# One address layout for the adjacency matrices of a graph and MoE kernel: half columns written into full rows

## The chip, the cores and the metric

The kernel runs on one core of a Trainium2 chip. The metric is the device time of one execution in microseconds (us). Three timed runs of the kernel before gave 2316.9, 2317.39 and 2327.94 us, median 2317.39 us.

## The reference

A graph of 3125 nodes with 256 features and 100000 weighted edges goes through four blocks. Cut to what matters here:

```python
# block 1, twice: aggregate over weighted edges
agg = segment_sum(edge_weight[:, None] * x[src], dst, num_segments=n)
x = gelu(layer_norm((x + agg) @ W + b))
# block 2: dense FFN with 4 small experts, top 2 gated (no edges)
# block 3: two GCN convolutions, over the edges with self loops
deg = segment_sum(ones, dst); dinv = rsqrt(deg)
out = segment_sum((x @ W)[src] * (dinv[src] * dinv[dst])[:, None], dst) + b
# block 4: 8 experts, top 2 gated, width 256 (no edges)
```

The edges come sorted by `dst`, and `dst` is drawn so that low node numbers have more edges.

## The kernel before, in words

The kernel turns the edge list into two dense matrices in device memory: `weight_matrix` (sums of edge weights from source node to destination node, plus one on the diagonal) and `count_matrix` (numbers of edges, plus one on the diagonal). Aggregation is then a dense matrix product on TensorE: all 25 tiles of 128 source nodes against a block of destination columns.

**The build.** The 3200 (padded) destination columns are made in 20 units of 160 columns (`UCOLS`). For each unit TensorE adds up one-hot products in PSUM (L1337, L1338), with one-hots that VectorE makes in batches (L980 to L985). ScalarE copies the sums in ten groups from PSUM to a staging buffer in SBUF (L560) and sets the PSUM banks back to zero (L564). GpSimd adds the diagonal (L821) and keeps a copy of the degree row (L823). Then SyncE (SP) issues two DMAs (L473), one for each matrix, of 128 partitions by 25 tiles by 160 columns of four bytes, 16000 bytes in each partition. There are two staging buffers, called halves: even units use half 0 and odd units half 1. Before ScalarE copies unit u into its half, `stage_free` has it wait until both DMAs of unit u-2 have landed. So unit u, its diagonal, its write and unit u+2 form one loop.

**The streaming.** Three passes read the matrices back, two over the weights and one over the counts. A pass has 10 steps of 320 columns (`SUB`, which is two units side by side). The 25 tiles of a step come in five DMAs (L506, for the very first step L476) into a ring of five slots of 5 tiles each. A slot is loaded again as soon as TensorE has used it, and TensorE comes back to it four slots later. TensorE multiplies each tile, 128 by 320, into two PSUM banks (L1401); each fp32 product is two instructions in the trace, 100 instructions in a step.

In device memory the layout before is [step, half, partition, tile, 160]. A unit's write is one unbroken piece for each partition (16000 bytes). A ring load needs two pieces of 3200 bytes for each partition, one from each half, and the SBUF slot keeps the halves apart: [half, tile, 160]. The moving operand of L1401 is then two runs of 160 columns that lie 3200 bytes apart.

**Between the two.** After the last unit, SP writes it, waits for the writes, and loads the ring for step 1; step 0 has been loaded beforehand. ScalarE issues some 60 DMAs for the weights of the model (L600) once the first ring loads have landed. After that it turns the degrees into the scaling values (L608, GpSimd L830, L611), for which TensorE waits before it goes on with the first pass (L1460).

Of the kernel before, what the change touches and what calls it, by code (L numbers as in the profile page):

```python
# [16 lines left out]
F32 = mybir.dt.float32  # L17
# [3 lines left out]
ds = bass.ds  # L21

P = 128
NODES = 3125
TILES = -(-NODES // P)
# [7 lines left out]
SUPERS = TILES // SUPER  # L33
SCOLS = SUPER * P
SUB = SCOLS // 2
QUADS = 5
UNITS = TILES // QUADS
# [15 lines left out]
UCOLS = SUB // 2  # L53
# [59 lines left out]
def build_program(nc, a, out):  # L113
    with ExitStack() as ctx:
# [4 lines left out]
            return ctx.enter_context(nc.semaphore(name))  # L119


        weight_dram = nc.dram_tensor("weight_matrix", [2 * SUPERS, 2, P, TILES, UCOLS], F32).ap()
        count_dram = nc.dram_tensor("count_matrix", [2 * SUPERS, 2, P, TILES, UCOLS], F32).ap()


        x_nodes = sb("x_nodes", [P, TILES, D])
        act_a = sb("act_a", [P, TILES, D])
        act_c = sb("act_c", [P, KD, PADDED])
        wide = sb("wide", [P, 18400])
        ring = wide[:, 0:8000].rearrange("p (a h b c) -> p a h b c", a=UNITS, h=2, b=QUADS)  # L130
        act_b = wide[:, 8000:14400].rearrange("p (t f) -> p t f", t=TILES)
        work = wide[:, 14400:18400]
        dinv_row = sb("dinv_row", [P, PADDED])
# [11 lines left out]
        cols = sb("cols", [P, 32])  # L145
# [64 lines left out]
        ps = ctx.enter_context(nc.psum_tensor("ps", [P, 8, 512], F32))  # L210
# [37 lines left out]
        stage = [wide[:, half * ROWS * UCOLS:(half + 1) * ROWS * UCOLS].rearrange("p (r c) -> p r c", r=ROWS) for half in range(2)]  # L248
# [210 lines left out]
        def _(sp):  # L459
# [9 lines left out]
            stage_end(sp, 1)  # L469

            def write(u2, half):
                for matrix, rows_of, written in ((weight_dram, slice(0, TILES), weights_written), (count_dram, slice(TILES, 2 * TILES), counts_written)):
                    sp.dma_start(matrix[ds(u2, 1), half, :, :, :].rearrange("a p t c -> (a p) t c"), stage[half][:, rows_of, :]).then_inc(written[half], 16)  # L473

            def first_unit(q):
                sp.dma_start(ring[:, q, :, :, :], weight_dram[0, :, :, q * QUADS:(q + 1) * QUADS, :].rearrange("h p t c -> p h t c")).then_inc(ring_ready[q], 16)  # L476
            with sp.Fori(0, BUNITS // 2 - 1) as u2:
                for half in range(2):
                    sp.wait_ge(unit_complete, u2 * 2 + half + 1)
# [15 lines left out]
            for k in range(PASSES):  # L495
                matrix = weight_dram if k < 2 else count_dram
                if k == 0:
                    for half in range(2):
                        sp.wait_ge(weights_written[half], 16 + 16 * BUNITS // 2)
                if k == 2:  # L500
                    for half in range(2):
                        sp.wait_ge(counts_written[half], 16 + 16 * BUNITS // 2)
                with sp.Fori(1 if k == 0 else 0, 2 * SUPERS) as u:
                    for q in range(UNITS):
                        sp.wait_ge(ring_used, (k * 2 * SUPERS + u) * UNITS + q + 1)
                        sp.dma_start(ring[:, q, :, :, :], matrix[ds(u, 1), :, :, q * QUADS:(q + 1) * QUADS, :].rearrange("a h p t c -> p (a h) t c")).then_inc(ring_ready[q], 16)  # L506
                if k == PASSES - 1:

                    sp.wait_ge(ffn_out, SUPERS)
                    for e in range(MOES):  # L510
                        sp.dma_start(moe_w2[:, e, :, :], a["L1_ffn_w2"][e].rearrange("(k p) n -> p k n", p=P)).then_inc(moe_w2_loaded, 16)
# [773 lines left out]
        def _(pe):  # L1285
# [98 lines left out]
            def stream(k, s, sub, q):  # L1384

                features = (act_a, act_b, act_b)[k]
                u = (k * SUPERS + s) * 2 + sub
# [10 lines left out]
                    pe.wait_ge(gcn_in, SUPER + (q + 1) * SUPER)  # L1398
                for t in range(QUADS):
                    for h in range(KD):  # L1400
                        i = nc.tensor.matmul(ps[:, 2 * sub + h, 0:SUB], features[:, q * QUADS + t, h * P:(h + 1) * P], ring[:, q, :, t, :],  # L1401
                                             start=q == 0 and t == 0, stop=q == UNITS - 1 and t == QUADS - 1)
                i.then_inc(ring_used, 1)

# [235 lines left out]
```

## Time and profile before

| | value |
|---|---|
| profiled execution | 2316.9 us, span 2315.2 us |
| granted TensorE clock, mean | 0.946 of full speed |
| TensorE busy | 2043.1 us (88%) |
| VectorE busy | 967.8 us (42%) |
| ScalarE busy | 579.4 us (25%) |
| GpSimd busy | 327.0 us (14%) |
| DMA | 70912 packets, 221.10 MB |
| build of the matrices | about 115 us to 729 us |
| first step of the first pass starts | 727.08 us |

The profile is of one execution. A share of busy time is a mean over stages with different limits: here the build has every engine partly busy, and the stages after it have TensorE nearly always busy. Idle time of an engine is listed with the instruction that ended it. "issue" in the chain of waits is time in which an engine waited for nothing that the trace shows. ACTq and SPq are the instruction queues of ScalarE and SyncE, from which they issue DMAs.

### The profile page before, as it was taken

The page shows a single profiled execution, that of the slowest core. Times are in us where ns is not written, and L with a number is a line of the kernel's source. Part 1 is how long each engine was busy: PE and PEld are TensorE (multiplying, and loading weights), DVE is VectorE, ACT ScalarE, POOL GpSimd, SP SyncE. Part 2 cuts the span into 40 slices and gives each one's busy share as a digit, 9 for nine tenths or more (in the row PEclk, how much of TensorE's full clock was granted, in tenths as well). Part 3 has the DMA queues.
Part 4 walks back from the last instruction along what each step waited for, and adds up shares of the span by engine and source line. Part 5 has one row for each costly group of instructions (what it writes and reads, how often), then busy time and mean ns, then how long its engine had stood idle before and what let it go on. Part 6 is the DMA issues. An engine that isn't in the chain of part 4 may idle for free.

```text
span 2315.2 us, 32368 instructions
## 1 busy us (share of the span) xinstructions
PE 2043.1 (88%) x11135; PEld 1584.2 (68%) x11136; DVE 967.8 (42%) x1977; ACT 579.4 (25%) x833; POOL 327.0 (14%) x158
## 2 busy tenths in 40 slices
PE   1688588777666899999999989999999999999997
PEld 1488477777665677777777766656777767777776
DVE  5999598978781011111332332221322233222222
ACT  0014356667663200000101112330000012222221
POOL 2007363445651000000000000000000000000000
PEclk7799799989888899999999998999999998999999
DMA  2000333443348544444434420004344330000000
GB/s 76 1 0 0 142 142 148 171 177 142 142 171 318 147 136 139 140 141 139 128 114 127 122 90 0 0 0 120 122 127 119 122 101 1 12 12 0 11 11 10
DMA packets 70912, 221.10 MB, mean 96 GB/s; under 512 B 10300, under 2 KB 27354, under 8 KB 65754
## 3 DMA queue, kind: packets, MB, share of 16 engines
q1 hardware_dynamic: 56554, 213.41, 26.7%
q10 hardware_dynamic: 14320, 7.18, 1.3%
q8 instruction: 25, 0.41, 0.1%
q14 instruction: 13, 0.11, 0.0%
HBM read 135.45 MB, written 85.12 MB: 95 GB/s over the span
## 4 chain that ended last, share of the span: by engine, by line
issue 57%; PE 25%; DVE 7%; POOL 3%; DMA 3%; ACT 2%; ACTq 1%; DVEq 1%; SPq 0%; POOLq 0%
PE ps L1570 8%; PE ps L1418 8%; PE ps L1337 6%; DVE act_c L985 3%; DMA count_matrix<-wide 3%; POOL wide L821 2%; PE ps L1338 2%; ACT wide L560 1%; PE ps L1312 1%; ACT ps L564 1%; POOL dinv_row L823 1%; DVE act_c L980 1%; ACTq L552 1%; PE ps L1594 1%; DVE wide L1274 0%
## 5 line engine op out<-in xcount | busy, mean ns | idle before, releaser
L1337 PE MATMUL ps<-early,act_c 128*128 128x200 bf16 x3600 | 464.4, 258 | 159.4 <-ACT ps L564 87.3
L1401 PE MATMUL ps<-wide 128*128 128x320 f32 x2000 | 545.3, 433 | 0.0
L1401 PEld LDWEIGHTS ps<-wide 128*128 128x128 f32 x2000 | 378.4, 190 | 153.5 <-issue 0.3
L1337 PEld LDWEIGHTS ps<-early,act_c 128*128 128x128 bf16 x3600 | 338.7, 100 | 189.8 <-issue 184.3
L1338 PE MATMUL ps<-early,act_c 128*128 128x208 bf16 x1200 | 313.0, 261 | 0.0
L821 POOL TENSOR_TENSOR wide<-wide,ident 128x128 f32 (+3 forms) x80 | 242.4, 3058 | 372.0 <-ACT ps L564 371.1
L985 DVE TENSOR_TENSOR act_c<-act_c,pair_tab 128x1024 bf16<-128x1024 bf16 x450 | 282.4, 679 | 0.0
L1401 PE MATMUL ps<-wide,act_a 128*128 128x320 f32 x1000 | 274.0, 436 | 2.1 <-ACTq L585 2.1
L1401 PEld LDWEIGHTS ps<-wide,act_a 128*128 128x128 f32 x1000 | 191.6, 192 | 81.9 <-issue 4.7
L560 ACT COPY wide<-ps 128x816 f32<-128x816 f32 x200 | 167.3, 837 | 283.5 <-PE ps L1338 192.0
L1274 DVE SCALAR_TENSOR_TENSOR wide<-ps,small,wide 128x256 f32<-128x256 f32 x200 | 82.0, 477 | 267.5 <-PE ps L1418 267.4
L1082 DVE TENSOR_TENSOR wide<-ps,rows 128x1280 f32<-128x1280 f32 x10 | 14.9, 1492 | 419.3 <-PE ps L1418 419.3
L1570 PE MATMUL ps<-act_a,wide 128*128 (+1 forms) x640 | 189.7, 452 | 0.0
L835 POOL TENSOR_TENSOR small<-small 128x5 f32<-128x5 f32 x25 | 29.2, 1166 | 1099.5 <-DVE small L1070 1099.5
L1418 PE MATMUL ps<-early,act_c 128*128 128x256 f32 x800 | 182.1, 383 | 2.3 <-DVEq L1276 2.3
L1418 PEld LDWEIGHTS ps<-early,act_c 128*128 128x128 f32 x800 | 153.8, 193 | 28.0 <-issue 2.7
L564 ACT ACTIVATE ps<-ones 128x816 f32<-128x816 f32 x200 | 170.6, 853 | 6.4
L738 ACT ACTIVATE act_c<-ps,cols 128x320 f32<-128x320 f32 x160 | 84.3, 527 | 322.7 <-PE ps L1570 322.7
L1570 PEld LDWEIGHTS ps<-act_a,wide 128*128 128x128 f32 x640 | 126.0, 199 | 54.4 <-issue 11.2
L981 DVE TENSOR_TENSOR early<-rows 128x1600 bf16<-128x1600 bf16 x150 | 146.8, 979 | 0.0
L980 DVE TENSOR_TENSOR act_c<-rows,pair_tab 128x1024 bf16<-128x1024 bf16 x150 | 102.0, 680 | 93.3 <-PE ps L1338 91.9
L1338 PEld LDWEIGHTS ps<-early,act_c 128*128 128x128 bf16 x1200 | 119.9, 100 | 1.7
(195 smaller groups left out, 1318.5 us busy)
## 6 DMA issues: line engine op xcount, KB each, us to landing
wide<-weight_matrix SPq DMA_DIRECT2D x100, 800.0 KB, 4.5
weight_matrix<-wide SPq DMA_DIRECT2D x20, 2000.0 KB, 6.2
count_matrix<-wide SPq DMA_DIRECT2D x20, 2000.0 KB, 10.8
wide<-count_matrix SPq DMA_DIRECT2D x50, 800.0 KB, 4.4
x_nodes<-in_x_dram ACTq DMA_DIRECT2D x1, 3072.0 KB
out_dram<-x_nodes SPq DMA_DIRECT2D x4, 640.0 KB
early<-in_L_ffn_w_dram SPq DMA_DIRECT2D x8, 256.0 KB, 5.3
wide<-in_L_ffn_w_dram SPq DMA_DIRECT2D x8, 256.0 KB, 4.5
```

Of the source, the lines that this page charges most:

```text
L560: act.copy(stage[half][:, :, k * GCOLS:(k + 1) * GCOLS].rearrange("p r (b j) -> p b r j", b=GROUP), group_ps.rearrange("p b (r j) -> p b r ...
L564: act.activation(group_ps, zero, ACT.Copy, scale=0.0).then_inc(acc_free, 1)
L738: act.activation(moe_h[e % 2][:, m, half * SUB:(half + 1) * SUB], ps[:, m * 2 + half, 0:SUB], ACT.Gelu, bias=moe_b1[:, e, m:m + 1]).then_i ...
L821: pool.tensor_tensor(part, part, eye, ALU.add).then_inc(pool_chain, 1)
L980: dve.tensor_tensor(hot_lane[:, slot, 0], for_each(lane_wide, P), of_pairs(pair_tab[:, 0, first], P), ALU.is_equal).then_inc(lane_made, 1)
L981: dve.tensor_tensor(hot_key[:, slot, :, 0:WCOLS, :], for_each(key_wide, WCOLS), of_pairs(pair_key[:, first], WCOLS), ALU.is_equal)
L985: i = dve.tensor_tensor(hot_lane[:, slot, part], hot_lane[:, slot, 0], of_pairs(pair_tab[:, part, first], P), ALU.mult)
L1337: nc.tensor.matmul(weights, hot_lane[:, slot, part, two, :, k], hot_key[:, slot, two, 0:WCOLS, k], start=False, stop=True, skip_group_chec ...
L1338: nc.tensor.matmul(counts, hot_lane[:, slot, 0, two, :, k], hot_key[:, slot, two, :, k], start=False, stop=True, skip_group_check=True).th ...
L1401: i = nc.tensor.matmul(ps[:, 2 * sub + h, 0:SUB], features[:, q * QUADS + t, h * P:(h + 1) * P], ring[:, q, :, t, :], start=q == 0 and t = ...
L1418: i = nc.tensor.matmul(tile_ps(bank, t), src_t[:, h, t * P:(t + 1) * P], w[:, h, :], start=h == 0, stop=h == KD - 1)
L1570: i = nc.tensor.matmul(ps[:, m * 2 + half, 0:SUB], moe_w1[:, e, k, m * P:(m + 1) * P], act_a_t[:, k, nodes(s, half)], start=k == 0, stop=k ...
```

## The change

The matrices in device memory get the layout [step, partition, tile, 320], and a ring slot gets [tile, 320]. A ring load is then one piece of 6400 bytes for each partition, and the moving operand of L1401 is one run of 320 columns. A unit's write goes into half of each row: 25 pieces of 640 bytes for each partition, which lie 1280 bytes apart in device memory. No instruction is added, removed or moved; bytes are the same.

```diff
-        weight_dram = nc.dram_tensor("weight_matrix", [2 * SUPERS, 2, P, TILES, UCOLS], F32).ap()
-        count_dram = nc.dram_tensor("count_matrix", [2 * SUPERS, 2, P, TILES, UCOLS], F32).ap()
+        weight_dram = nc.dram_tensor("weight_matrix", [2 * SUPERS, P, TILES, SUB], F32).ap()
+        count_dram = nc.dram_tensor("count_matrix", [2 * SUPERS, P, TILES, SUB], F32).ap()
...
-        ring = wide[:, 0:8000].rearrange("p (a h b c) -> p a h b c", a=UNITS, h=2, b=QUADS)
+        ring = wide[:, 0:8000].rearrange("p (a b c) -> p a b c", a=UNITS, b=QUADS)
...
             def write(u2, half):
+                cols = slice(half * UCOLS, (half + 1) * UCOLS)
                 for matrix, rows_of, written in ((weight_dram, slice(0, TILES), weights_written), (count_dram, slice(TILES, 2 * TILES), counts_written)):
-                    sp.dma_start(matrix[ds(u2, 1), half, :, :, :].rearrange("a p t c -> (a p) t c"), stage[half][:, rows_of, :]).then_inc(written[half], 16)
+                    sp.dma_start(matrix[ds(u2, 1), :, :, cols].rearrange("a p t c -> (a p) t c"), stage[half][:, rows_of, :]).then_inc(written[half], 16)
...
-                sp.dma_start(ring[:, q, :, :, :], weight_dram[0, :, :, q * QUADS:(q + 1) * QUADS, :].rearrange("h p t c -> p h t c")).then_inc(ring_ready[q], 16)
+                sp.dma_start(ring[:, q, :, :], weight_dram[0, :, q * QUADS:(q + 1) * QUADS, :]).then_inc(ring_ready[q], 16)
...
-                        sp.dma_start(ring[:, q, :, :, :], matrix[ds(u, 1), :, :, q * QUADS:(q + 1) * QUADS, :].rearrange("a h p t c -> p (a h) t c")).then_inc(ring_ready[q], 16)
+                        sp.dma_start(ring[:, q, :, :], matrix[ds(u, 1), :, q * QUADS:(q + 1) * QUADS, :].rearrange("a p t c -> (a p) t c")).then_inc(ring_ready[q], 16)
...
-                        i = nc.tensor.matmul(ps[:, 2 * sub + h, 0:SUB], features[:, q * QUADS + t, h * P:(h + 1) * P], ring[:, q, :, t, :],
+                        i = nc.tensor.matmul(ps[:, 2 * sub + h, 0:SUB], features[:, q * QUADS + t, h * P:(h + 1) * P], ring[:, q, t, :],
```

On SP, at the end of the build (the write of unit 18, the first ring loads, the write of unit 19, and the first ring load of the loop), the program before has these rows; the figures are the shape of the device-memory side of each DMA in elements of four bytes:

```order
L473 DMA weight_matrix<-wide 128x4000
L473 DMA count_matrix<-wide 128x4000
L476 DMA wide<-weight_matrix 128x2x800 x5
L473 DMA weight_matrix<-wide 128x4000
L473 DMA count_matrix<-wide 128x4000
L503 UNCONDITIONAL_BRANCH
L503 ISA
L506 ISA
L506 DMA wide<-weight_matrix 128x2x800
```

and the changed program has, in the same place (its lines are one further down):

```order
L474 DMA weight_matrix<-wide 3200x1x160
L474 DMA count_matrix<-wide 3200x1x160
L477 DMA wide<-weight_matrix 128x1600 x5
L474 DMA weight_matrix<-wide 3200x1x160
L474 DMA count_matrix<-wide 3200x1x160
L504 UNCONDITIONAL_BRANCH
L504 ISA
L507 ISA
L507 DMA wide<-weight_matrix 128x1600
```

The order is the same. Each write has 3200 pieces instead of 128, and each ring load 128 pieces instead of 256.

## Rows read from the trace of the kernel before

**Rows 1.** The page: busy tenths of TensorE in 40 slices of the span
```profile
PE   1688588777666899999999989999999999999997
```

**Rows 2.** Pieces of the chain of waits in the build: start us, us, what
```profile
249.27 11.23 DMA count_matrix<-wide
...
643.08 10.57 DMA count_matrix<-wide
653.88 3.43 ACTq L552
...
675.43 10.83 POOL wide L821 x3
686.26 3.58 POOL dinv_row L823
690.47 10.68 DMA count_matrix<-wide
```

**Rows 3.** The tile count_matrix: who waited for its DMAs (us, times)
```profile
  ACT wide L560: 90.1, 5
```

**Rows 4.** Timeline of ScalarE: first copies of units 11, 17, 18, last of 11
```profile
507.08 0.84 ACT L560 COPY wide<-ps 128x816 f32<-128x816 f32 x1 [9.89 <-PE ps L1338]
...
525.53 0.84 ACT L560 COPY wide<-ps 128x816 f32<-128x816 f32 x1
...
657.36 0.84 ACT L560 COPY wide<-ps 128x816 f32<-128x816 f32 x1 [14.07 <-issue]
...
675.00 0.84 ACT L560 COPY wide<-ps 128x816 f32<-128x816 f32 x1 [0.79 <-PE ps L1338]
```

**Rows 5.** Timeline of SP's queue: count writes of units 9 and 16, first ring loads
```profile
495.04 0.38 SPq L473 DMA_DIRECT2D count_matrix<-wide  x1
...
652.94 0.38 SPq L473 DMA_DIRECT2D count_matrix<-wide  x1
...
710.90 2.95 SPq L476 DMA_DIRECT2D wide<-weight_matrix  x5
```

**Rows 6.** DMA queue q1: whole span; then 642.5 to 654.5 us, writes of unit 15
```profile
q1 hardware_dynamic: 56554, 213.41, 26.7%
...
DMA packets 320, 4.61 MB, mean 384 GB/s; under 512 B 32, under 2 KB 32, under 8 KB 32
q1 hardware_dynamic: 320, 4.61, 90.2%
```

**Rows 7.** DMA from 2234 to 2238 us, a store of output rows of 1024 bytes
```profile
DMA packets 636, 0.63 MB, mean 159 GB/s; under 512 B 16, under 2 KB 636, under 8 KB 636
q1 hardware_dynamic: 636, 0.63, 47.6%
```

**Rows 8.** DMA from 2.9 to 19 us: input rows, q10 1024 bytes, q1 512
```profile
q10 hardware_dynamic: 3087, 3.14, 61.4%
q1 hardware_dynamic: 2436, 1.20, 27.6%
```

**Rows 9.** Timeline of ScalarE's queue: an issue behind a load of 3072 rows
```profile
1.64 5.61 ACTq L531 DMA_DIRECT2D x_nodes<-in_x_dram  x1
```

**Rows 10.** Timeline of PE, L1401: the first step, and from 821 us
```profile
727.08 28.85 PE L1401 MATMUL ps<-wide,act_a 128*128 128x320 f32 x100 [2.09 <-ACTq L585]
...
821.79 28.43 PE L1401 MATMUL ps<-wide,act_a 128*128 128x320 f32 x105
```

**Rows 11.** The chain of waits from 1927 us: L1570, 320 columns in one run; L1418, 256
```profile
1927.08 4.31 PE ps L1570 x16
1931.39 4.32 PE ps L1418 x20
```

**Rows 12.** The page, DMA issues: KB each, us to landing
```profile
wide<-weight_matrix SPq DMA_DIRECT2D x100, 800.0 KB, 4.5
```

**Rows 13.** Timelines of the transition: last issue of L600, PE L1460
```profile
775.14 1.12 ACTq L600 DMA_DIRECT2D router<-in_L_ffn_router_w_dram  x2
...
788.61 5.48 PE L1460 MATMUL ps<-act_c,ones 128*128 128x128 f32 x32 [9.26 <-ACT act_c L611]
```

## Prediction

> **What bounds the kernel now.** I read the slices of the page first [rows 1]. From the 14th slice on (after about 750 us) TensorE has digit 8 or 9 in every slice but the last; in the build before that it has 5 to 8. So the kernel has two parts with different limits: after 727 us, where the first pass begins [rows 10], TensorE sets the time, and up to there some loop through several engines does.
>
> The second view is the chain of waits [rows 2]. In the build it passes six times through a write of the count matrix, 10.5 to 11.2 us each: those of units 0, 7, 11, 13, 15 and 17 (the first and the last two stand in the rows). In the last part one turn of the loop can be read off: the write of unit 15 is issued at 643.08 and takes 10.57, ScalarE loads its counts (3.43), starts unit 17 at 657.36, GpSimd adds the diagonal (10.83 and 3.58), and the write of unit 17 is issued at 690.47, 47.4 us after that of unit 15. The third view is who waited for the count matrix: ScalarE, 90.1 us in 5 waits [rows 3], one of them the 14.07 us before unit 17 [rows 4]. So the writes are not background traffic: six of 20 stand on the path, and every microsecond added to them there is a microsecond of the kernel.
>
> **The ring loads and TensorE's operand (the parts that get simpler).** A load of 800 KB lands 4.5 us after its issue [rows 12]. A slot's ten products are 20 instructions of 0.269 us (below), 5.4 us, and TensorE returns to a slot after the four others, 21.5 us. The load has 17 us to spare, so a quicker one is worth nothing. That is also why I count nothing for 128 pieces of 6400 bytes instead of 256 of 3200.
>
> TensorE reads two runs of 160 columns now, and one run of 320 after. The trace has both. L1401, with two runs, does 105 instructions in 28.43 us [rows 10]; less the modelled 0.43 of the last one that is 28.00 / 104 = 269.2 ns from one to the next. L1570, whose 320 columns lie in one run, does 16 in 4.31 us, 269.4 ns [rows 11]. The gap between the runs costs nothing, so closing it saves nothing: 3000 instructions by 0.
>
> **The writes (the part that gets harder).** What does a packet of 640 bytes cost? The trace before has none in this direction, but it has rows on both sides.
> - 16000 bytes: in 12 us there are 320 packets in 90.2% of the time of 16 engines, 173.2 us [rows 6]. 32 of them are under 512 bytes (semaphore writes, counted as nothing); the other 288 took 601 ns each.
> - 1024 bytes, stored to device memory: 47.6% of 16 engines' 4 us is 30.5 us for 636 packets, 16 of them such small ones: 49.1 ns each for the rest [rows 7].
> - 512 and 1024 bytes, loaded: 27.6% of 16 by 16.1 us over 2436 packets is 29.2 ns; 61.4% over 3087 is 51.2 ns [rows 8].
>
> A straight line through the two stores has 0.0369 ns for each byte and 11.4 ns for each packet, and gives 35.0 ns for 640 bytes. The loads give 29.2 + (128/512) x 22.0 = 34.7 ns. I take 35.0. A unit's two writes are 6400 packets, 400 on each engine, so 14.0 us, against 16 packets of 601 ns now, 9.6 us. That is **4.4 us more for each unit**, and the landing moves from 10.7 to about 15 us. The bounds: if the packet cost were only its share of bytes, nothing is added; if 640 bytes cost as much as 1024 do, it is 400 x 49.1 = 19.6 us, 10.0 more.
>
> The Trainium skill has two rules here, and both are kinder than the rows. "DMA: Bandwidth & Descriptors", section Specifications, puts the smallest transfer at line rate at 512 bytes; by it 640 bytes would cost no more per byte and the sum would be zero. Its section "Why small descriptors are slow" charges about 3 cycles beside one for each 32 bytes; by that 640 bytes cost 23 instead of 20, an estimate of 15% more than the bytes alone, or 1.4 us for each unit. The trace does not agree with either: at 1024 bytes, twice the threshold, a packet took 49.1 ns where its share of the 16000-byte packet is 38.5.
>
> Can the pieces be made fast enough? While ScalarE's issue sat 5.61 us behind a load of 3072 rows [rows 9], those rows were being taken up, so some 550 pieces come in a microsecond or more; the engines finish 16 / 35.0 ns = 457 in a microsecond. The count write may be held in SP's queue for 5 to 6 us, but the weight write ahead of it keeps the engines busy for 7.0 us, so that delay is covered.
>
> **On which units it counts.**
> - The six of the chain: 6 x 4.4 = 26.4 us. Nothing else waits beside these writes, so I see no cover.
> - Odd units 3, 5 and 9 are near the chain. The count write of unit 9 is issued at 495.04; landed and noticed 12 us later, it is in time for the copy at 507.08, and the idle time before that is put down to TensorE [rows 4, 5]. TensorE can fill the four pairs of banks (`SETS`) before it needs ScalarE, about 6 us ahead at 2 us a pair, and ScalarE, which took 18.45 us over nine groups of unit 11 (507.08 to 525.53) where copy and zeroing alone are 1.66 each, has 3.5 us in hand. I take 1 us for all three; the ends are 0 and 3 x 4.4 = 13.2.
> - Even units have room. The write of unit 16 (652.94) would now stand behind unit 15's until about 658 and land at about 672.5; ScalarE turns to unit 18 at 675.00 now and 4.4 later then [rows 4, 5].
> - Units 17 and 18 together keep the engines for 28 us from 690.5, so the first ring loads are issued at about 719.5 instead of 710.90 [rows 5] and are in by about 730. The first pass starts at 727.08 now, at 731.5 by this shift, and needs the slots one after another. Nothing.
> - The transition. TensorE idles 9.26 us before L1460, because the degrees come late: ScalarE issues model weights until 776.3, and only then goes to L608, L830 and L611 [rows 13]. Those loads share the engines with the last unit's write. That write occupies them 4.4 us longer, and its 6400 pieces stand in front of ScalarE's requests. I take 4 us; the ends are 0, if the issues catch up, and 10.
>
> Sum: 26.4 + 1 + 4 = 31 us. The profiled execution took 2316.9 us, its span 2315.2 and 1.7 around it; it is also the lowest of the three, and the median of 2317.39 is 0.5 above. So 2317.4 + 31 = 2348 us. By the 1.4 us of the Trainium skill ("DMA: Bandwidth & Descriptors", "Why small descriptors are slow") it would be about 2328, an estimate.
>
> **The rivals.**
> - *Forecast: packets by the straight line, six writes on the path.* 2348 us, own range 2336 to 2364 (3.0 to 5.5 us for each write, the small terms between their ends). Chance 0.66.
> - *Not slower: the packet cost is hidden.* An engine may overlap the fixed part of one 640-byte packet with the next, as the pieces here lie in one SBUF run. The place is the same six writes, the price 0 to 1.6 us each: 2317 to 2329. It ends within 0.5% if 25 packets take under about 700 ns, 28 ns each (11.6 us over seven terms is 1.65 us a unit, 103 ns on each of 16 rows). For it speaks that the transfer's SBUF side is unchanged; against it the 49.1 and 29.2 ns, measured in streams that were full. Chance 0.13. The line-rate rule of the Trainium skill ("DMA: Bandwidth & Descriptors", Specifications) would make this the outcome.
> - *Much slower: a packet of 640 bytes to alternate places costs as a 1024-byte one or more, or the pieces come too slowly.* 10.0 for each unit: 60 on the six, 7 on unit 9 since its room is used up, 10 at the transition, 2394 us. For it speaks that no row has stores with gaps in device memory; against it that two kinds of loads and one of stores fall on one line. Chance 0.17.
> - *Faster: TensorE gains from the single run.* L1418, with 256 columns, takes 4.32 / 20 = 216 ns [rows 11], so a column costs 53.2 / 64 = 0.83 ns and 320 of them 266; at most the other 3 ns of the 269.2 could go, so 9.6 us over 3000 instructions, and only if the writes add nothing: 2308 us. Rows 10 and 11 show the same cadence for both forms. Chance 0.03, and 0.01 for anything else.
>
> **How the numbers follow.** The likeliest case gives 2348. The range for 8 in 10 takes in the forecast's own range, reaches down to the upper end of the hidden case and up into the third: 2328 to 2380. About 0.5% is what a measurement of this kernel can tell from no change, 11.6 us. Faster by more: 0.04. Within it: 0.11, nearly all of the hidden case and a little of the forecast's low side. Slower: 0.85.
>
> **What would show it right or wrong.** Packets of queue q1 rise from 56554 [rows 6] by 128000 - 5120 for the writes and fall by 19200 for the loads, to about 160000. The DMA view of one late unit shows about 35 ns for each packet, and the count write lands 15 us after the weight write's issue. The chain of waits has count writes of 14 to 15 us at units 0, 7, 11, 13, 15, 17, and ScalarE's waits for the matrix grow from 90 to about 112 us. From issue to issue units 15 and 17 stand 51.8 us apart instead of 47.4. L1401 keeps 269 ns. TensorE's idle time before L1460 grows to about 13 us. The prediction is wrong in its main step if the write lands after 12 us or less, wrong in size if it lands after 18 or more, and wrong in its view of TensorE if 100 instructions of L1401 take other than 26.9 us at full clock.

## The result and the profile after

The changed kernel took 2348.24 us, median of four runs (2342.54, 2347.54, 2348.95, 2361.11), beside 2318.74 us for the kernel before on the same chip (four runs, 2316.9 to 2327.94). The ratio is 1.0127, 95% interval 1.0078 to 1.0177: slower by 29.5 us. The forecast was 2348 us. Medians in this document are of all timed runs, while a ratio takes of each kernel only the runs within about 1.5% of its fastest, which on the third chip below is often half of them or fewer.

The profiled execution took longer than all four, 2370.09 us, so its rows tell more loss than the median has. The page of it has these lines, to be laid beside the same lines of before [rows 1, 6, 12] and the table of before:

```profile
span 2367.8 us, 32365 instructions
...
PE 2045.9 (86%) x11132; PEld 1586.3 (67%) x11136; DVE 966.1 (41%) x1977; ACT 579.5 (24%) x833; POOL 347.7 (15%) x158
...
PE   1698448877675889999999997999999999999997
...
DMA packets 174592, 221.10 MB, mean 93 GB/s; under 512 B 10300, under 2 KB 155354, under 8 KB 174554
...
q1 hardware_dynamic: 160234, 213.41, 28.6%
...
wide<-weight_matrix SPq DMA_DIRECT2D x100, 800.0 KB, 4.3
...
count_matrix<-wide SPq DMA_DIRECT2D x20, 2000.0 KB, 13.8
```

The bytes are the same, the packets of q1 are the 160000 that were forecast, and a ring load still lands after 4.3 us. TensorE's busy time is 2.8 us more, with the loss in its gaps. Of the engines' busy times only GpSimd's has grown much: 347.7 us of busy time instead of 327.0, for the same 158 instructions.

The chain of waits in the build (start us, us, what) now passes through eight count writes, of which these are all:

```profile
250.59 13.88 DMA count_matrix<-wide
...
335.96 13.36 DMA count_matrix<-wide
...
446.59 13.88 DMA count_matrix<-wide
...
500.50 13.72 DMA count_matrix<-wide
...
553.55 13.65 DMA count_matrix<-wide
...
607.32 13.41 DMA count_matrix<-wide
...
658.76 13.53 DMA count_matrix<-wide
...
709.80 13.42 DMA count_matrix<-wide
```

Against the rows of before [rows 2] two things differ. Each write takes 13.4 to 13.9 us instead of 10.5 to 11.2. And they are the writes of units 0, 2, 6, 8, 10, 12, 14 and 16, eight even units, where the chain of before took six, mostly odd ones. The view of who waited for count_matrix says the same from ScalarE's side, 154.3 us in 7 waits against 90.1 in 5 [rows 3]:

```profile
  ACT wide L561: 154.3, 7
```

GpSimd's timeline differs too, from unit 2 on. First the kernel before, units 0, 2 and 19 (start us, us, what, idle before and its releaser):

```profile
190.80 57.51 POOL L821 TENSOR_TENSOR wide<-wide,ident 128x128 f32 x4 [111.80 <-ACT ps L564]
...
287.69 13.15 POOL L821 TENSOR_TENSOR wide<-wide,ident 128x64 f32 x4 [37.15 <-ACT ps L564]
...
726.93 1.28 POOL L821 TENSOR_TENSOR wide<-wide,ident 128x32 f32 x4 [27.26 <-ACT ps L564]
```

and the changed kernel, unit 2 and after it unit 3:

```profile
292.19 42.64 POOL L822 TENSOR_TENSOR wide<-wide,ident 128x64 f32 x4 [40.64 <-ACT ps L565]
...
335.54 1.28 POOL L822 TENSOR_TENSOR wide<-wide,ident 128x32 f32 x4 [0.44 <-POOL dinv_row L824]
```

Four small additions take 1.28 us in one place and 42.64 or 57.51 in another. The windows say what ran beside them (window; busy us and instructions of PE, PEld, DVE, ACT, POOL; clock, DMA share, GB/s): in the kernel before at unit 0 and at unit 19, and then in the changed kernel at unit 2,

```profile
192.00:247.00 55.00, 42.77 (x453) 39.69 (x451) 55.00 (x97) 16.92 (x20) 55.00 (x1) 0.96 0.00 0
...
726.00:729.00 3.00, 1.92 (x4) 1.36 (x5) 0.00 (x0) 2.12 (x3) 1.54 (x5) 0.70 0.10 11
```

```profile
293.00:333.00 40.00, 32.27 (x344) 30.13 (x341) 40.00 (x71) 16.93 (x20) 40.00 (x1) 1.00 0.00 0
```

Where GpSimd is slow, VectorE is busy for 55.00 of 55 us with 97 instructions, and 40.00 of 40 with 71; nothing else is at its limit, and no DMA moves. Where it is quick, at unit 19, VectorE has nothing to do.

But a full VectorE alone does not make the difference between 13.15 and 42.64 us at unit 2. In the kernel before VectorE is busy without a gap there as well, and GpSimd gets through, with about 3.6 us for each operation. The window, one of its operations, and two instructions of VectorE, the first in the stretch where GpSimd stands still and the second beside the operation shown:

```profile
288.00:304.00 16.00, 14.36 (x154) 13.41 (x153) 16.00 (x27) 10.14 (x12) 16.00 (x5) 1.00 0.00 0
...
297.17 3.68 POOL L821 TENSOR_TENSOR wide<-wide,ident 128x96 f32 x1
...
245.18 0.17 DVE L982 TENSOR_TENSOR early<-rows 128x64 bf16<-128x64 bf16 x1
...
296.85 0.41 DVE L982 TENSOR_TENSOR early<-rows 128x64 bf16<-128x64 bf16 x1
```

VectorE makes its one-hots in batches of six instructions, one batch in 3.4 to 3.6 us. At unit 2 GpSimd finishes one operation in each batch, at the end of L982, which then takes 0.33 to 0.41 us instead of 0.17 or 0.18. At unit 0 the first of its operations does not end before VectorE has run dry, at 247.16 us (and at unit 2 of the changed kernel likewise, at 333.7). VectorE's next instruction after that is

```profile
271.12 0.69 DVE L980 TENSOR_TENSOR act_c<-rows,pair_tab 128x1024 bf16<-128x1024 bf16 x1 [23.96 <-PE ps L1338]
```

The 10.83 and 3.58 us of GpSimd in the chain of before [rows 2] are four such turns, one batch of VectorE each. I call a unit *held* when its diagonal step takes over 20 us. The kernel before has one held unit here (0), the changed one two (0 and 2).

The spans differ by 52.6 us (2315.2 and 2367.8). By the start of unit 0's write 1.3 are lost, by the last copy of unit 19 (725.03 before, 763.78 after) 37.4 more, from there to the start of the first pass 10.9, and after it 2.9.

### The profile page after: what moved, and what is told of

The parts are those of the page before. It is cut to its first block, busy times and chain, and to the rows that moved or that the text cites. A ratio compares the mean times of both kernels' runs of the same rounds, so it can differ in the third digit from the quotient of the medians.

```text
span 2367.8 us, 32365 instructions
## 1 busy us (share of the span) xinstructions
PE 2045.9 (86%) x11132; PEld 1586.3 (67%) x11136; DVE 966.1 (41%) x1977; ACT 579.5 (24%) x833; POOL 347.7 (15%) x158
## 4 chain that ended last, share of the span: by engine, by line
issue 58%; PE 23%; DVE 5%; DMA 5%; POOL 4%; ACT 3%; ACTq 1%; SPq 0%; DVEq 0%; POOLq 0%
PE ps L1571 7%; PE ps L1419 7%; DMA count_matrix<-wide 5%; PE ps L1338 4%; POOL wide L822 3%; ACT wide L561 2%; DVE act_c L986 2%; PE ps L1339 1%; ACTq L553 1%; PE ps L1313 1%; ACT ps L565 1%; POOL dinv_row L824 1%; PE ps L1595 1%; DVE act_c L981 1%; DVE wide L1275 0%
## 5 line engine op out<-in xcount | busy, mean ns | idle before, releaser
L822 POOL TENSOR_TENSOR wide<-wide,ident 128x128 f32 (+3 forms) x80 | 269.7, 3401 | 389.5 <-ACT ps L565 388.2
L982 DVE TENSOR_TENSOR early<-rows 128x1600 bf16<-128x1600 bf16 x150 | 147.2, 981 | 0.0
```

What stands on the lines that cost most here:

```text
L822: pool.tensor_tensor(part, part, eye, ALU.add).then_inc(pool_chain, 1)
L982: dve.tensor_tensor(hot_key[:, slot, :, 0:WCOLS, :], for_each(key_wide, WCOLS), of_pairs(pair_key[:, first], WCOLS), ALU.is_equal)
```

## The experiments

The chips are not alike. The result above is called that of the first chip here. The second series ran on the second chip (which may be the same one; the record does not number the first), and the first and third series on the third. The kernel before took 2319 to 2321 us on the first and second and 2411 to 2413 on the third, so every kernel is compared with runs of the kernel before beside it. In the third series the four kernels of the first were run again, with the edits shown there.

### The change again, and its operand alone (first series)

The first is the changed kernel as it is, on this chip. The second is the kernel before with one edit, so that TensorE reads one run of 320 columns (ring slots are then read in another order, so the products are of other elements):

```diff
-    ring[:, q, :, t, :],
+    wide[:, (q * QUADS + t) * SUB:(q * QUADS + t + 1) * SUB],
```

> The changed kernel once more, for a second profile. In its first profile (2370.1 us, against a median of 2348.2) GpSimd stood still for 42.6 us at unit 2, where the kernel before took 13 us there, and the chain of waits then went through the writes of the even units, eight of them. Theory A (a loop that may lock on even or on odd units, by chance of that first stall): a profile near 2348 us shows a short GpSimd step at unit 2 and writes of odd units on the chain, about six or seven of 13.7 us. Theory B (the longer write itself moves the loop to the even units in every run): GpSimd again takes about 40 us at unit 2 and the even units are on the chain. Both expect a median of 2343 to 2355 us and 34 ns for each 640-byte packet.

> The kernel before with its transfers untouched; only TensorE's moving operand in L1401 is one run of 320 columns of the ring slot instead of two runs of 160 (the columns of a product are then mixed up among the tiles of the slot, which changes the values and no amount of work). My prediction: the cadence stays at 269 ns and the time is that of the kernel before, ratio 0.998 to 1.002. Rival (the single run speeds TensorE up): up to 3 ns less for each of 3000 instructions, 9 us, ratio 0.996 or lower.

The kernel before took 2413.41 us (17 runs, 2379.82 to 2435.76), the changed one 2436.16 (12 runs), ratio 1.0064 (1.0006 to 1.0122). The operand's kernel took 2433.35 in six runs from 2366.76 to 2444.41, too wide for a ratio; its median is 19.9 us above that of the kernel before, where the third series will find 6.1 below. So on this chip some 20 us between two medians can come from nothing, and the change's 22.8 here is hardly more. Neither median is where it was expected, the change's at 2343 to 2355 us and the operand's at 0.998 to 1.002 of before. The operand's profile has the loop of this chip, with the writes of before: nine count writes on the chain, of 10.51 to 11.20 us, and eight held units. The first two are

```profile
191.13 57.54 POOL L821 TENSOR_TENSOR wide<-wide,ident 128x128 f32 x4 [111.90 <-ACT ps L564]
...
288.15 42.63 POOL L821 TENSOR_TENSOR wide<-wide,ident 128x64 f32 x4 [37.24 <-ACT ps L564]
```

and the others step down from 38.0 to 25.3 us. So a held unit 2 needs no small pieces: the layout of before has it too, 42.63 and 42.64 us. In the changed kernel's profile here seven units are held, among them not unit 2 (13.16 us), and the chain has eight even units' writes of 13.34 to 13.87 us all the same. Theory A, which expected odd units after a short step at unit 2, fell; theory B expected the even units, but with unit 2 held. From one held unit to the next the changed kernel needs 3.8 us more than the operand's kernel does (units 14 to 16: 61.6 and 57.8; units 12 to 14: 65.6 and 61.8). That is the price of a turn between two held units, free of the question of how many are held.

### A delay without small pieces, and an earlier write (first series)

The third kernel keeps the layout of before and puts a spare DMA of 21 tiles per partition between a unit's two writes. The fourth lets the write begin before GpSimd copies the degree row.

```diff
+SPARE = 21
...
+    if matrix is weight_dram:
+        sp.dma_start(spare_dram[ds(u2, 1), half, :, :, :].rearrange("a p t c -> (a p) t c"), stage[half][:, 0:SPARE, :]).then_inc(spare_written[half], 16)
...
+    act.wait_ge(spare_written[half], u2 * 16 + 16)
```

```diff
-    pool.tensor_copy(degree_part[...], stage[half][:, 2 * TILES, :]).then_inc(pool_chain, 1)
-    pool.wait_ge(pool_chain, count(5))
+    pool.wait_ge(pool_chain, count(4))
     pool.sem_inc(unit_complete, 1)
+    pool.tensor_copy(degree_part[...], stage[half][:, 2 * TILES, :]).then_inc(pool_chain, 1)
+    pool.wait_ge(pool_chain, count(1))
```

> The kernel before with its 16000-byte pieces, plus a third DMA between the two writes of each unit that stores 21 of the 25 weight tiles once more to a spare tensor: 13440 bytes a partition, 8 packets of about 505 ns on each engine, 4.0 us more before the count write lands. Theory A (the change costs what it adds to the landing of the writes): the time is that of the changed kernel less 0.4 us a unit, about 2343 us, and count writes of 14 to 15 us on the chain. Rival (the number of pieces costs by itself: SP's issue takes 4 to 12 us in the changed kernel, and ScalarE's and SP's requests stand behind 6400 pieces): this kernel gains well less than 20 us over the kernel before, 2325 to 2335.

> The kernel before, with GpSimd reporting a unit complete before it copies the degree row instead of after. The write is issued 3.6 us earlier in each unit on the chain, and the copy (3.6 us) runs beside it. Theory A (GpSimd's steps and the write are in series with ScalarE's copies in the last ten units and at unit 7): 5 to 6 units by 3.6 us, 18 to 22 us less, about 2298 us. Rival (the loop is held by VectorE's one-hots, and the chain only passes through the writes where they tie): under 5 us less.

The delay: 2464.55 us, ratio 1.0238 (1.0171 to 1.0305), nine count writes of 14.0 to 14.7 us on the chain. The earlier write: 2408.24 us, ratio 0.9874 (0.9781 to 0.9967), from three of seven runs; its median is only 5.2 us below, where 18 to 22 were expected. Both signs agree with a loop through the write. But neither theory of the delay came true: its median is 51.1 us above that of the kernel before, where the change's was 22.8, at a landing 0.7 to 0.8 us longer. The count writes of three turns that end in a held unit in all three profiles tell more than the medians (us from one to the next):

| units | operand (writes of before) | change | delay |
|---|---|---|---|
| 4 to 6 | 67.9 | 71.4 | 71.9 |
| 12 to 14 | 61.8 | 65.6 | 67.5 |
| 14 to 16 | 57.8 | 61.6 | 61.3 |

By turns the delay costs 3.5 to 5.7 us and the change 3.5 to 3.8. So a longer landing with large pieces only costs what the change does, or a little more, and nothing is left that the number of pieces would have to explain. The profiled delay reaches the first pass 48.1 us after the profiled change; the write of its unit 4 already comes 24.1 us later, since unit 2 is held there and not in the change. For the medians this is not shown.

### GpSimd out of the loop (second series)

The same edit, in the kernel before and in the changed one: GpSimd signals the unit at once and neither adds the diagonal nor copies the degree row (so both are left out of what is computed). The kernel before ran again beside them.

```diff
-    pool.tensor_tensor(part, part, eye, ALU.add).then_inc(pool_chain, 1)    # in a loop, four or two of them
-    pool.tensor_copy(degree_part[...], stage[half][:, 2 * TILES, :]).then_inc(pool_chain, 1)
-    pool.wait_ge(pool_chain, count(5))
     pool.sem_inc(unit_complete, 1)
```

> The kernel before once more, for a profile on the chip of these runs. Theory C (what decides the build is whether GpSimd finds a gap in VectorE's work): where the time is well above 2317 us, GpSimd's diagonal step takes 25 to 40 us at several units, the writes of two units follow each other within 3 us, and the units come in pairs about 58 to 66 us apart; at 2317 us they come 47 to 50 us apart and the step takes 8 to 16 us.

> The kernel before without GpSimd's work in the build: it only passes the signals on. Left out are the ones on the diagonals and the degree row, so the values differ. Theory C: with GpSimd out of the loop VectorE never waits for a staging buffer, and the build is its 511 us of work after 115 us: the first pass starts at 635 to 660 us instead of 727, the time is 2235 to 2260 us, and it is steady from run to run and from chip to chip. Rival (the loop is held by the write and ScalarE's copies, GpSimd's work only fills gaps): 15 us a pair of units at the most in the last ten units, about 2270 or more.

> The changed kernel with the same part left out. Theory C: a unit's write (15 us to its landing) now fits beside the 33 us in which ScalarE copies two units, so the six to eight writes leave the path; what stays is the transition, 0 to 15 us. The difference to the kernel before without GpSimd's work is at most 15 us, against 29.5 between the two whole kernels. Rival (the write costs wherever it stands): six writes by 4.1 us or more, 25 us or more of difference.

The kernel before again: 2319.1 us, ratio 0.9985 (0.9963 to 1.0006). Its profile repeats the first one: unit 0 held and no other, and count writes of units 0, 7, 11, 13, 15 and 17 on the chain, 47 to 51 us from one to the next in the last four, as expected for such a time. Without GpSimd's part: 2251.13 us, ratio 0.9691 (0.9659 to 0.9723); the changed kernel without it: 2263.25 us, ratio 0.9746 (0.9719 to 0.9773). The change now costs 12.1 us, not 29.5. Who waited for whom, in the kernel before without GpSimd's part and then in the changed one (us in total, times, the longest; ScalarE from 100 to 720 us):

```profile
ACT wide L560 <- PE ps L1327: 215.2, 113, 24.4
```

```profile
ACT wide L561 <- PE ps L1328: 218.1, 112, 24.4
```

ScalarE waits for TensorE only, in 113 and 112 waits of 1.9 us on average, and for no write at all. The first pass begins at 662.82 and 665.72 us, 2.9 apart, where the whole kernels' passes were 49.7 apart. What is left of the loss is elsewhere, in TensorE's idle time before L1450:

```profile
722.98 5.55 PE L1449 MATMUL ps<-act_c,ones 128*128 128x128 f32 x32 [6.31 <-ACT act_c L611]
```

```profile
730.33 5.46 PE L1450 MATMUL ps<-act_c,ones 128*128 128x128 f32 x32 [12.42 <-ACT act_c L612]
```

It grows by 6.1 us, the transition's term of the forecast. The profiled spans differ by 7.1 us in all (2250.2 and 2257.3), the profile of the changed kernel being of its fastest run, and the medians by 12.1. The times came as theory C expected, except that the first pass starts some 3 us after the end of its range of 635 to 660 us. That they are steady holds for runs on this chip (2242 to 2260 us and 2259 to 2265); on another they were not tried. The rival that the write and ScalarE's copies alone would hold the loop, even without GpSimd, fell.

### The diagonal by ScalarE (second series)

A whole version, in the layout of before: after ScalarE has set a PSUM group to zero it copies the ones of the diagonal into PSUM, TensorE adds onto them, and ScalarE copies the degree row too. Eight matmuls at the start prepare the banks for that. GpSimd has no part in the build unless the edges are out of order. Its core, cut:

```diff
+    def eye_into(tile, col, first_bank):
+        dst = ps[:, first_bank:first_bank + GROUP, 0:2 * WCOLS].rearrange("p b (k t j) -> p b k t j", k=2, j=WIN)[:, :, :, ds(tile, 1), :]
+        src = ident[:, col:col + GCOLS].rearrange("p (b j) -> p b j", j=WIN).unsqueeze(2).broadcast_to([P, GROUP, 2, WIN])
+        act.activation(dst.rearrange("p b k a j -> p b k (a j)"), src, ACT.Copy).then_inc(acc_free, 1)
...
-    act.activation(group_ps, zero, ACT.Copy, scale=0.0).then_inc(acc_free, 1)
+    act.activation(group_ps, zero, ACT.Copy, scale=0.0).then_inc(acc_zero, 1)
...
+    act.activation(degree_part[...], stage[half][:, 2 * TILES, :], ACT.Copy).then_inc(unit_complete, 1)
```

> A whole version (all values computed) with the layout of before: ScalarE puts the ones of the diagonal into PSUM after it has zeroed a pair of banks (one small operation of about 0.25 us for each group, 2.5 us a unit) and copies the degree row itself; GpSimd has no part in the build. ScalarE has then about 20 us a unit, close under VectorE's 20 to 25. Theory C: 2240 to 2275 us, 2 to 3% faster than the kernel before. Rival (ScalarE becomes the bound, since every group now waits for zeroing and diagonal before TensorE may go on): no gain, 2300 or more.

It took 2253.65 us, ratio 0.9707 (0.9679 to 0.9735): faster than the kernel before by 2.9%, as expected. The added instruction is L553, in ScalarE's timeline late in the build:

```profile
603.07 0.21 ACT L553 ACTIVATE ps<-ident 128x32 f32<-128x32 f32 x1
603.20 0.85 ACT L591 ACTIVATE ps<-ones 128x816 f32<-128x816 f32 x1
603.99 0.83 ACT L585 COPY wide<-ps 128x816 f32<-128x816 f32 x1
604.72 0.20 ACT L553 ACTIVATE ps<-ident 128x32 f32<-128x32 f32 x1
```

It takes 0.13 to 0.14 us from its start to the next instruction's. The first pass begins at 659.53 us, 67.6 earlier than in the profile of before [rows 10].

### The same four on the third chip once more (third series)

> The changed kernel again, since all kernels, the one before too, were some 90 us slower on the chip of the first series and GpSimd's step was held up there in all of them. On a chip where the kernel before takes about 2320: median 2345 to 2355. Theory C (the write's 4.1 us more are paid at each turn of a loop whose length is set by ScalarE's copies, GpSimd and the write): the writes on the chain of waits times 3.1 us (13.8 instead of 10.7 to the landing), plus the time that GpSimd's steps grow, plus what TensorE waits for the first ring loads, add up to the difference of the two builds. If GpSimd is held up at unit 2 again (about 40 us), the profiled time is above 2360; if not, at 2340 to 2350.

> The kernel before with only TensorE's moving operand of L1401 read as one run of 320 columns (the columns of a product are mixed up among the tiles of the slot, which changes the values and no amount of work). Prediction: cadence 269 ns, ratio 0.997 to 1.003. Rival: up to 3 ns less for each of 3000 instructions, ratio 0.996 or lower.

> The kernel before with its large pieces, plus a third DMA between the two writes of each unit that stores 21 of the 25 weight tiles once more: 4.0 us more before the count write lands. Theory A (the change costs what it adds to the landing): within 10 us of the changed kernel, 2338 to 2352 where the kernel before takes 2320. Rival (the number of pieces costs by itself, in SP's and ScalarE's queues): under 2335, well below the changed kernel.

> The kernel before, with GpSimd reporting a unit complete before it copies the degree row. Theory C: the write of each unit on the chain is issued 3.6 us earlier, 5 to 6 units, so 18 to 22 us less (ratio about 0.991), unless GpSimd is then held up at other units, which can eat it. Rival (VectorE's one-hots hold the loop): ratio 0.998 or more.

Beside 2411.27 us for the kernel before: the change 2441.52 (no ratio), the operand 2405.22, ratio 1.0017 (0.9963 to 1.0071), the delay 2463.42, ratio 1.0291 (1.0224 to 1.0359), the earlier write 2387.33, ratio 0.9815 (0.9724 to 0.9905; two of its six runs). The delay is again 52.2 us above and not within 10 us of the change, so that expectation failed twice. The earlier write is 23.9 us below, about what was expected, but with 5.2 in the first series its size is not known. The change's profile (2413.82 us, unit 2 held) lies above 2360 us, as expected for that case. The sum of theory C for it is 9 x 3.1 us for the writes, 56.8 for GpSimd's steps (299.2 us instead of 242.4) and 11.1 for the ring, 95.8 in all, and the first pass starts 87.9 us later than in the first profile of before; in the change's first profile the same sum is 63.0 and the start 49.7 later. So it is too high by 8 to 13 us: not all that GpSimd loses is on the path. The operand alone changes nothing that these runs can tell, and its L1401, from 760 to 1000 us, has

```profile
916.88 54.00 PE L1401 MATMUL ps<-wide,act_a 128*128 128x320 f32 x200
```

that is (54.00 - 0.43) / 199 = 269.2 ns from one to the next, the figure of before.

All profiles together, with the number of held units and the side of the loop near its end (on which units the last four count writes of the chain are):

| kernel, chip | held units | last four writes on the chain | first pass starts | span |
|---|---|---|---|---|
| before, first | 1 | odd | 727.1 | 2315.2 |
| before again, second | 1 | odd | 725.6 | 2317.3 |
| change, first | 2 | even | 776.8 | 2367.8 |
| operand, third (third series) | 3 | odd | 761.9 | 2360.3 |
| operand, third (first series) | 8 | even | 830.3 | 2431.9 |
| change, third (third series) | 5 | even | 815.0 | 2411.9 |
| change, third (first series) | 7 | even | 838.1 | 2435.4 |
| delay, third (third series) | 4 | even | 826.6 | 2428.9 |
| delay, third (first series) | 8 | even | 886.2 | 2488.3 |
| earlier write, third (third series) | 2 | odd | 730.1 | 2320.7 |
| earlier write, third (first series) | 7 | even | 813.6 | 2406.4 |
| no GpSimd, before / change; diagonal by ScalarE | 0 | none | 662.8 / 665.7; 659.5 | 2250.2 / 2257.3; 2251.0 |

From the start of the first pass to the end all take 1587 to 1602 us. Within one kernel the runs with more held units are the longer ones: the operand's two profiles differ by 71.6 us in five units, the earlier write's by 85.7 in five, 14 and 17 us for each. I take this for the reason why the third chip's runs spread over 44 to 107 us for one kernel; for runs without a profile it is not shown.

The table also tells more of the even units. All five profiles with a longer landing (change and delay) end on even units, with two to eight units held. Of the six with the landing of before four end on odd units, two of them although unit 2 was held (the operand and the earlier write of the third series), and only the two with seven and eight held units end on even ones. So a held unit 2 is neither needed for the even loop nor enough for it. The longer landing seems to be what keeps the loop there, and many held units seem to do it too; no run separates the two.

The medians of the change lie 22.8 and 30.3 us above those of before there, 29.5 on the first chip.

## Why the prediction was right, and where it was not

**The loop.** Right, and the experiments bear on it: a write stands in series with GpSimd, ScalarE and the next unit, so that what is added to it is paid (the delay), and what is taken from it is gained (the earlier write, in sign). With GpSimd's part gone, no copy waits for a write, and the build lost only 2.9 us by the change. The prediction had the loop right, but not its units: it expected the writes of units 0, 7, 11, 13, 15 and 17 and 112 us of waits, and the profile has eight even units and 154.3 us. It also took GpSimd's 10.83 us in the loop as a given.

**The packet.** Forecast 35.0 ns for 640 bytes. The two writes of unit 6, from 445.9 to 460.9 us (the first row in 40 slices of 0.375 us):

```profile
GB/s 0 0 0 191 357 365 367 360 352 360 350 338 329 335 329 336 333 335 329 333 333 336 333 335 331 338 331 338 333 335 336 333 333 336 335 184 20 5 0 0
DMA packets 6432, 4.10 MB, mean 273 GB/s; under 512 B 32, under 2 KB 6432, under 8 KB 6432
...
q1 hardware_dynamic: 6432, 4.10, 91.4%
```

0.914 x 16 x 15.0 = 219.4 us over 6400 packets is 34.3 ns. The straight line was right within 2%. Both kinder rules of the Trainium skill ("DMA: Bandwidth & Descriptors", Specifications and "Why small descriptors are slow") do not fit this row. From the 601 ns of a 16000-byte packet the first gives 24.0 ns for 640 bytes and the second 27.6, both estimates.

**From packets to the landing: the first mis-sized term.** 4.4 us more for each unit were forecast; the chain's writes grew from about 10.7 to about 13.6 us, 2.9 more, and with the weight write's longer issue ahead of them (0.55 instead of 0.38) 3.1. A late turn, from the write of unit 14 to that of unit 16, takes 709.80 - 658.76 = 51.0 us against the 47.4 of before [rows 2]: 3.6 more, where 4.4 were forecast. The step that was off is "400 packets on each engine, so 14.0 us": each packet does take 34.3 ns, which makes 13.7, but the bulk flowed at about 335 GB/s, 4.1 MB in some 12.2 us and with its ramps 12.8. So an engine has more than one packet in hand at a time. In a busy stretch, from 709 to 724 us, the packets' times even add up to more than the time of 16 engines:

```profile
q1 hardware_dynamic: 7240, 4.61, 102.9%
```

The second rival of the forecast named this overlap; it was worth some 0.9 of the 4.4 us.

**The count of writes: the second.** Six times 4.4 is 26.4. In the profiled run eight were on the chain. Eight times 3.1 to 3.6 is 25 to 29: the sum of the forecast came right with its two factors off in opposite directions. And this profile lost 52.6 us in all, not 29.5. For the timed runs, whose median is 22 us below the profiled one, I have no profile, so their count is not known. That their median lies within a microsecond of the forecast is luck: both factors were off, by some 20 to 30% each. The pair without GpSimd's part says the same. There no write is on the chain and the change still costs 12.1 us, where the forecast had 4 outside the loop. If those 12.1 are in the whole kernels too, which is not shown, the loop's share of the 29.5 is about 17 us and not 27.

**SP's issue.** The count write held SP for 3.96 us in the middle of the build and 12.15 at its end, against 0.38 before [rows 5]:

```profile
445.95 0.55 SPq L474 DMA_DIRECT2D weight_matrix<-wide  x1
446.59 3.96 SPq L474 DMA_DIRECT2D count_matrix<-wide  x1
...
772.37 2.52 SPq L477 DMA_DIRECT2D wide<-weight_matrix  x5
775.52 12.15 SPq L474 DMA_DIRECT2D count_matrix<-wide  x1
```

As forecast, it is covered by the weight write in the middle of the build.

**The first ring loads: "Nothing" was wrong in the profiled run.** They were issued at 772.37 us (rows above), after the write of unit 18 had landed, and TensorE waited for them, 13.01 us where it had waited 2.09 [rows 10]:

```profile
776.76 28.71 PE L1402 MATMUL ps<-wide,act_a 128*128 128x320 f32 x100 [13.01 <-DMA wide<-weight_matrix]
805.30 5.84 PE L1451 MATMUL ps<-ones,dinv_row 128*128 128x1 f32 x50
813.63 18.27 PE L1402 MATMUL ps<-wide,act_a 128*128 128x320 f32 x60 [2.49 <-DMA wide<-weight_matrix]
841.40 5.41 PE L1461 MATMUL ps<-act_c,ones 128*128 128x128 f32 x32 [9.49 <-ACT act_c L612]
```

That is the 10.9 us between the last copy and the first pass. The forecast's rows had the loop on odd units, where unit 18's write is early. With the loop on even units, unit 18's write comes late: its count write was issued at 757.56 us, 6 us before unit 19's last copy; in the kernel before it was at 700.14, 25 us before. The loads wait for it. The operand's kernel, in the layout of before and with an even loop, waits 11.04 us; with an odd loop (third series) it waits 2.09. So most of the wait belongs to the even loop. The changed kernel's three profiles have 13.01 to 14.36 and the delay's two 15.0 and 15.2, so 2 to 4 us more go with the longer landing.

**The transition.** 4 us forecast. The idle time before L1461 is 9.49 against 9.26 [rows 13], so 0.2 here, presumably since TensorE had already stood still for the ring; in the second series, where it had not, 6.1. Inside the bounds of 0 to 10.

**The operand and the ring loads.** Right: 95 instructions from 874.51 us took 25.73, so (25.73 - 0.43) / 94 = 269.1 ns, and the operand alone gave 1.0017 (0.9963 to 1.0071).

```profile
874.51 25.73 PE L1402 MATMUL ps<-wide,act_a 128*128 128x320 f32 x95
```

**What was overlooked.** GpSimd's row of 57.51 us was there in the trace of before, and none of my views was of GpSimd by itself. Four operations of the same kind took 1.28 us elsewhere. Taking GpSimd's part out was worth 68 us (2319.1 to 2251.1), twice the change. In the profiles it also sets how far one run of a kernel lies from another: a unit is held or it is not.

**What stays open.** Why GpSimd gets its turn in each batch of VectorE in one execution and in none in the next, and so why the third chip needs 90 us more. That VectorE is what keeps GpSimd back is read from the rows; no run took VectorE's work away. Whether the longer landing itself makes the loop even. Why the delay's median lies 51 to 52 us above that of before, where the change's lies 23 to 30. Whether the new layout would still cost 12 us with the diagonal made by ScalarE was not tried, though the pair without GpSimd suggests it. Where the 5 us lie by which the medians of that pair differ more than their profiles.

## What to carry to other kernels

Compare the shortest and the longest time of one kind of operation before you take any of its times as given: 1.28 and 57.5 us for four small additions were a sign of something worth more than the change that was studied. Ask of a DMA layout which side gets the small pieces and whether that side stands on a loop; here the loads' gain was worth nothing and the loop paid for each write. A sum of packet times over an engine came out above the time of the transfer (13.7 and 12.8 us), and the GB/s of its middle was the better measure. And where runs of one kernel spread by several per cent, compare single turns of the loop between profiles; here they agreed where the medians did not.

## What the runs showed of the hardware

Beside VectorE's batches of two-input instructions without a gap GpSimd's operations did one of two things. Either they took about 3.6 us each, one in each batch of six instructions (unit 2 of the kernel before), or none was finished for as long as VectorE went on: 55.00 us beside 97 instructions, and 40.00 beside 71. The same unit of the same kernel did the one in one execution and the other in the next (unit 2 of the changed kernel, 13.16 and 42.64 us). The Trainium skill ("SBUF — State Buffer", "SBUF: two separate sides" and "Who interferes with whom") says that a VectorE instruction with two inputs in SBUF and a GpSimd operation that reads SBUF exclude each other, and that whichever starts first keeps the other out for the whole instruction. The trace agrees that GpSimd is slow beside such instructions (1.28 us for four operations where VectorE is idle). But the wait here went over some hundred instructions, not to the end of one.

Packets of 640 bytes to device memory, 1280 apart, took 34.3 ns each and moved at about 335 GB/s; those of 16000 bytes took 601 ns each [rows 6]. The issue of a DMA of 3200 pieces behind another held SP's queue for 4 us (3.96 at unit 6), for 6 where the write of the unit before was still under way (6.04 at unit 17), and for 12.15 behind the ring loads at the end, against 0.38 us for 128 pieces.

One kernel took medians of 2319 us on the first chip, 2319 and 2321 on the second, and 2411 and 2413 on the third.
